# Attended values behind the score products: TensorE's round of a decoder layer put in a new order

## The reference, cut to what matters

```python
x = x + out(softmax(rope(q) @ rope(k).T / sqrt(8), causal) @ v)     # q, k, v from layernorm(x)
q2 = layernorm(x); s2 = (q2 @ wq) (ctx @ wk).T / dk                 # per head of 8, no softmax
y = layernorm(q2 + (s2 @ (ctx @ wv)) @ wo) * ln_g + ln_b
x = x + y
e = argmax(layernorm(x) @ centroids.T)                              # one expert per token
x = x + gated(expert_e(layernorm(x)))
```

## Time and profile before

| | us |
|---|---|
| median of three runs (lowest, highest) | 590.66 (588.89, 592.01) |
| span of the profiled execution, first to last instruction | 587.3 |
| TensorE busy (products) | 544.2 |
| VectorE busy | 486.7 |
| ScalarE busy | 490.9 |
| GpSimd busy | 423.8 |

### The profile page before, as it was taken

The page is one execution under the profiler, slowest core; times in us unless marked ns, Lnnn a source line. Parts: engine busy times, 40 slices in busy tenths (PEclk is TensorE's granted clock), DMA queues, the critical chain, the costliest instruction groups (busy, mean ns, idle before and its releaser), DMA issues.

```text
span 587.3 us, 25042 instructions
## 1 busy us (share of the span) xinstructions
PE 544.2 (93%) x7951; PEld 417.9 (71%) x7951; DVE 486.7 (83%) x1762; ACT 490.9 (84%) x1358; POOL 423.8 (72%) x820
## 2 busy tenths in 40 slices
PE   3889999999999999999999999998889999999994
PEld 2557676767666666666676667665688898899994
DVE  2887898999898989988999898986778777777773
ACT  2778788999888899888898889887688797899993
POOL 3334678888888888888888888777767666454553
PEclk9999999999999999999999999998999999999998
DMA  5521111123111132111221111111211222322210
GB/s 172 69 73 30 30 39 39 57 71 96 59 57 57 58 91 77 58 57 57 64 82 45 39 39 39 46 38 31 70 36 52 67 67 81 91 71 69 68 55 10
DMA packets 55182, 35.35 MB, mean 60 GB/s; under 512 B 14976, under 2 KB 50433, under 8 KB 55056
## 3 DMA queue, kind: packets, MB, share of 16 engines
q1 hardware_dynamic: 50160, 24.44, 15.2%
q0 software_dynamic: 4320, 8.66, 4.5%
q10 hardware_dynamic: 576, 0.66, 0.4%
HBM read 24.46 MB, written 9.74 MB: 58 GB/s over the span
## 4 chain that ended last, share of the span: by engine, by line
PE 79%; issue 6%; ACT 5%; DVE 5%; SPq 1%; POOL 1%; DVEq 1%; DMA 0%; POOLq 0%; ACTq 0%
PE side L946 9%; PE side L747 6%; PE quad L695 6%; PE quad L728 5%; PE quad L733 5%; PE side L808 5%; PE quad L931 4%; PE side L931 4%; PE side L676 4%; PE side L666 3%; PE side L844 3%; PE side L862 3%; PE quad L687 3%; PE side L778 2%; PE side L829 2%
## 5 line engine op out<-in xcount | busy, mean ns | idle before, releaser
L2026 POOL DMA_INDIRECT out<-yo,rb x71 | 70.1, 988 | 59.9 <-DVE yo L1767 53.1
L1055 ACT ACTIVATE ex<-qk,cf 128x512 f32<-128x512 f32 x128 | 85.3, 715 | 0.8
L946 PE MATMUL side<-w,hT 128*128 x568 | 76.7, 278 | 6.2 <-DVE hT L1561 4.7
L1419 DVE TENSOR_REDUCE mx<-quad 128x16 f32<-128x1024 f32 x64 | 75.3, 1218 | 6.6 <-PE quad L695 5.5
L1993 POOL DMA_INDIRECT expert_rows<-pay,sli x64 | 68.6, 1072 | 13.4 <-issue 12.6
L946 PEld LDWEIGHTS side<-w,hT 128*128 128x128 f32 x568 | 69.1, 192 | 9.0 <-issue 8.9
L1071 ACT ACTIVATE prob<-quad 128x1024 f32<-128x1024 f32 x64 | 62.3, 1030 | 1.5 <-PE quad L733 1.5
L1551 DVE TENSOR_SCALAR xh<-rb 128x128 f32<-128x128 f32 x71 | 26.0, 368 | 26.5 <-issue 22.5
L747 PE MATMUL side<-prob,vau 128*32 128x64 f32 x2048 | 41.7, 222 | 4.0 <-issue 2.4
L1168 ACT COPY w1b<-w 128x512 f32 x71 | 43.5, 615 | 0.0
L747 PEld LDWEIGHTS side<-prob,vau 128*32 128x32 f32 x2048 | 31.9, 110 | 10.2 <-issue 3.1
(11 more groups left out here) (270 smaller groups left out, 1641.1 us busy)
## 6 DMA issues: line engine op xcount, KB each, us to landing
rb<-expert_rows SPq DMA_DIRECT2D x71, 68.0 KB, 1.8
xin<-in_x SPq DMA_DIRECT2D x32, 128.0 KB
cin<-in_ctx SPq DMA_DIRECT2D x32, 128.0 KB
xr<-in_x SPq DMA_DIRECT2D x32, 128.0 KB, 2.1
w<-in_w1t SPq DMA_DIRECT2D x8, 256.0 KB
w<-in_w2t SPq DMA_DIRECT2D x8, 256.0 KB
out<-yo,rb POOLq DMA_INDIRECT x71
expert_rows<-pay,sli POOLq DMA_INDIRECT x64, 2.4
```

The lines of the kernel that those rows point to most:

```text
L946: last = mm(YB[u][:, 0:D], hT[u][:, c, :], w2[:, bass.ds(e, 1), c, :], start=c == 0, stop=c == FC - 1)
L1055: act(ex[g.par][:, i, :, :].rearrange("p a t -> p (a t)"), qk[g.par][:, :, :].rearrange("p a t -> p (a t)"), ACT.Copy, scale=own4[:, i:i + ...
L1419: v.tensor_reduce(mx[g.par][:, 2 * h_:2 * h_ + 2, :], quad[:, 2 * h_:2 * h_ + 2, :].rearrange("p r (h k) -> p r h k", k=SQ), AX.X, ALU.max ...
L2026: v.indirect_dma_start(out=o_rows, out_offset=bass.IndirectOffsetOnAxis(ap=number, axis=0), in_=yo[b.c % 4][:, :], in_offset=None, bounds_ ...
```

## The change

Every engine's round gets a new order, and the banks 4 to 7 get new tenants; the instructions of a round stay the same. On TensorE the attended values (64x64 tiles) stand between the score products and the Gram products (64x64 tiles); the two halves of the weighted values stand together at the end; `values` and `ctx_turned` run a round later, `ranks` a round earlier. On ScalarE the round is cut at another place (one more round, most steps one stage deeper), and the second half of `by_head` opens the round. On VectorE `weighted_turned` and `inverse` close the round in which the weighted values are made, and `place` does so for the ranks. GpSimd's two scatters stand side by side. SyncE's queue loads the context two rounds earlier. After the rounds, the steps that now run inside them are dropped, and two waits of the first expert blocks change places.

```diff
         BANK = {
...
+            "x1_turned": bank[5],
+            "cross_keys_values": bank[4],
+            "x_turned": bank[5],
+            "cross_queries": bank[7],
+            "values": bank[6],
+            "ctx_turned": bank[4],
+            "queries_keys": bank[5],
+            "max_rows": bank[7],
+            "projected": bank[6],
...
+            "attended": bank[5],
+            "values_keys0": bank[6],
+            "values_keys1": bank[7],
             "cross_output": bank[4],
+            "ranks": bank[6],
             "weighted": bank[7],
...
@@ SyncE
             def one(g):
-                stage(g, 2, load_ctx)
+                stage(g, 0, load_x)
+                stage(g, 0, load_ctx)
                 stage(g, 3, load_again)
-                stage(g, 0, load_x)
@@ TensorE, the table of waits, first entries of what the text speaks of
-                "attended": [(ac_t, "cT", 4), (ac_f, "xT", 4), (dv_t, "mt", 1), (ac_t, "A", -1)],
+                "attended": [(dv_f, "k2", 4), (ac_f, "xT", 4), (ac_t, "xT", 0), (ac_t, "A", -1)],
-                "x_turned": [(dv_t, "mt", -3), (ac_t, "A", -5), (ac_t, "cT", -1), (ac_f, "xT", -1)],
+                "x_turned": [(ac_t, "xT", -4), (ac_t, "A", -5), (dv_f, "k2", -1), (ac_f, "xT", -1)],
+                "ranks": [(dv_t, "mt", 3), (dv_t, "x1", 2), (ac_f, "V1", 4), (dv_r, "tot", -1)],
+                "weighted": [(dv_t, "mt", 0), (ac_s, "x", 0), (ac_t, "Q2", -2), (dv_a, "ot", -1)],
...
@@ TensorE
             def one(g):
                 stage(g, 4, max_scores)
-                stage(g, 2, x_turned)
                 stage(g, 6, x1_turned)
                 stage(g, 4, cross_keys_values)
-                stage(g, 8, ranks)
+                stage(g, 2, x_turned)
                 stage(g, 6, cross_queries)
-                stage(g, 2, ctx_turned)
+                stage(g, 3, values)
+                stage(g, 3, ctx_turned)
                 stage(g, 2, queries_keys)
-                stage(g, 6, attended)
                 stage(g, 4, max_rows)
                 stage(g, 5, projected)
                 stage(g, 4, scores)
+                stage(g, 6, attended)
+                stage(g, 4, values_keys)
                 stage(g, 6, cross_output)
-                stage(g, 4, values_keys)
+                stage(g, 7, ranks)
                 stage(g, 4, weighted, 0)
-                stage(g, 2, values)
                 stage(g, 4, weighted, 1)
@@ ScalarE
             def one(g):
+                stage(g, 3, by_head, (2, 3))
+                stage(g, 5, norm_x1)
+                stage(g, 6, squares)
+                stage(g, 1, norm_x)
+                stage(g, 5, x1_turned)
+                stage(g, 7, exp_affinity)
+                stage(g, 3, cross_keys_values)
+                stage(g, 1, x_turned)
+                stage(g, 5, cross_queries)
+                stage(g, 3, max_high)
+                stage(g, 2, values)
+                stage(g, 2, ctx_turned)
+                stage(g, 3, max_by_head)
+                stage(g, 6, token_ids)
+                stage(g, 2, by_head, (0, 1))
+                stage(g, 3, exp, 0)
                 stage(g, 5, attended)
-                stage(g, 3, exp, 0)
                 stage(g, 3, exp, 1)
-                stage(g, 0, norm_x)
-                stage(g, 4, norm_x1)
-                stage(g, 5, squares)
-                stage(g, 1, values)
-                stage(g, 0, x_turned)
-                stage(g, 5, token_ids)
-                stage(g, 4, x1_turned)
-                stage(g, 2, cross_keys_values)
-                stage(g, 4, cross_queries)
-                stage(g, 6, exp_affinity)
-                stage(g, 2, max_high)
-                stage(g, 0, ctx_turned)
-                stage(g, 1, by_head, (0, 1))
-                stage(g, 2, max_by_head)
-                stage(g, 1, by_head, (2, 3))
...
@@ VectorE, the new order
+                stage(g, 8, counted)
+                stage(g, 8, own_rank)
                 stage(g, 4, row_max, 0)
+                stage(g, 8, slots)
                 stage(g, 4, row_max, 1)
+                stage(g, 8, alpha)
                 stage(g, 5, turned_back)
+                stage(g, 7, scaled_scores)
                 stage(g, 8, slot_numbers)
                 stage(g, 7, x2_sum)
...
                 stage(g, 7, affinities)
                 stage(g, 7, stats_x2)
                 stage(g, 2, rotate)
                 stage(g, 7, largest)
+                stage(g, 5, x1_sum)
+                stage(g, 7, largest_at)
+                stage(g, 5, stats_x1)
+                stage(g, 7, first_of_them)
+                stage(g, 4, own_head)
+                stage(g, 7, choose)
+                stage(g, 2, partners)
                 stage(g, 6, y_sum)
+                stage(g, 7, place)
+                stage(g, 1, stats_x)
+                stage(g, 4, weighted_turned)
+                stage(g, 4, inverse)
...
@@ GpSimd
             def one(g):
+                stage(g, 1, std_x)
+                stage(g, 6, std_y)
                 stage(g, 4, divide)
-                stage(g, 6, std_y)
+                stage(g, 2, rotated)
                 stage(g, 3, max_low)
-                stage(g, 0, std_x)
                 stage(g, 7, scatter_rows, 0)
-                stage(g, 4, std_x1)
                 stage(g, 7, scatter_rows, 1)
                 stage(g, 6, std_x2)
+                stage(g, 6, row_scalars)
+                stage(g, 5, offset_x1)
+                stage(g, 4, std_x1)
                 stage(g, 5, gain)
-                stage(g, 1, rotated)
-                stage(g, 5, offset_x1)
                 stage(g, 6, scaled_affinity)
-                stage(g, 6, row_scalars)
```

More of the change, by code:

```diff
@@ L432, in decoder_kernel @@
             "max_scores3": bank[3],
-            "x_turned": bank[6],
-            "x1_turned": bank[4],
-            "cross_keys_values": bank[7],
-            "ranks": bank[5],
-            "cross_queries": bank[4],
-            "ctx_turned": bank[6],
-            "queries_keys": bank[7],
-            "max_rows": bank[4],
-            "projected": bank[5],
-            "attended": bank[6],
+            "x1_turned": bank[5],
[7 more added lines that the diff above has]
+            "projected": bank[6],
             "scores0": bank[0],
@@ L446, in decoder_kernel @@
             "scores3": bank[3],
+            "attended": bank[5],
+            "values_keys0": bank[6],
+            "values_keys1": bank[7],
             "cross_output": bank[4],
-            "values_keys0": bank[5],
-            "values_keys1": bank[6],
+            "ranks": bank[6],
             "weighted": bank[7],
-            "values": bank[4],
         }
@@ L464, in decoder_kernel @@
         CT = 2
-        SETUP = bank[5]
+        SETUP = bank[7]
         EARLY_AT = (NG - 4, NG - 1, NG, NG + 1, NG + 2, NG + 3)
@@ L585, in _ @@
                 "max_scores3": [(ac_a, "e1", -1), (dv_s, "m1", -1)],
[L586 to L598 removed]
+                "x1_turned": [(ac_t, "A", -1), (dv_f, "k2", 3), (ac_f, "xT", 3), (ac_t, "xT", -1)],
+                "cross_keys_values": [(dv_t, "y1", -3), (ac_t, "cT", 0), (ac_t, "kv", -1)],
+                "x_turned": [(ac_t, "xT", -4), (ac_t, "A", -5), (dv_f, "k2", -1), (ac_f, "xT", -1)],
+                "cross_queries": [(dv_a, "ot", 1), (dv_t, "mt", 1), (ac_s, "x", 1), (ac_t, "Q2", -1)],
+                "values": [(dv_r, "tot", -5), (dv_t, "mt", -2), (dv_t, "x1", -3), (ac_f, "V1", -1)],
+                "ctx_turned": [(ac_t, "kv", -1), (dv_t, "y1", -4), (ac_t, "cT", -1)],
+                "queries_keys": [(ac_f, "xT", 0), (ac_t, "xT", -4), (ac_t, "A", -5), (dv_f, "k2", -1)],
+                "max_rows": [(ac_t, "Q2", -2), (dv_a, "ot", -1), (dv_t, "mt", -1), (ac_s, "x", -1)],
+                "projected": [(ac_f, "V1", 2), (dv_r, "tot", -3), (dv_t, "mt", 0), (dv_t, "x1", -1)],
                 "scores0": [(dv_s, "m0", 0), (ac_a, "e0", -1)],
@@ L923, in hidden @@
                 if b.c == 1:
-                    wait(pe, ac_t, NG - 3, "A")
                     wait(pe, dv_a, NG - 1, "ot")
-                    wait(pe, dv_t, NG - 1, "mt")
+                    wait(pe, dv_r, NG - 4, "tot")
                 if b.c < 2:
@@ L941, in second @@
                 if b.c == 1:
-                    wait(pe, dv_r, NG - 4, "tot")
+                    wait(pe, ac_t, NG - 3, "A")
                 wait_b(pe, "act_relu", b.n)
@@ L957, in _ @@
             x1_turned(g30)
-            ranks(g28)
             transposed(Block(1))
@@ L1214, in _ @@
             act(ea1[0][:, 0:1], half[:, 0:1], ACT.Exp)
-            rounds(one, NG + 2)
+            rounds(one, NG + 3)
             g28, g29, g30, g31 = (Group(NG - k) for k in (4, 3, 2, 1))
@@ L1227, in step @@
                 return e2
-            attended(g29)
-            exp(g31, 0)
-            exp(g31, 1)
             e0, e1 = first_two(Block(0))
@@ L1466, in own_head @@
                 v.tensor_tensor(mt2[g.par][:, :, :, :],
```

(5 more changed lines are left out.)

37 lines of the change are left out of this document (3 added, 34 removed).

## The result

| | kernel before | kernel after |
|---|---|---|
| median of 5 runs, us | 590.0 (588.9 to 592.0) | 605.1 (602.5 to 605.8) |
| span of the profiled execution, us | 587.3 | 600.2 |

The ratio is 1.0246 with a 95% interval of 1.0224 to 1.0268: 15 us slower where 12.8 us faster was forecast. 605 lies outside the range of 565 to 592.

The account below looks back on a forecast made before the run. TensorE was taken to bound the kernel before, GpSimd the changed one. Gains of 10.6 (steady rounds), 2.1 (outer rounds) and 0.9 (end), less 0.8 (start), make 12.8 us: 590.7 to 578 us, range 565 to 592.

Parts of the forecast that it names:

- all three loads keep about a round of lead: SyncE's queue: context load moves to round 0, its buffer is freed one product later; cost put at nothing.
- start term: First rounds: no 3.16 us context wait, but later values and context and more ScalarE work; net loss 0.8 us, bounds 3.
- 11.95 us: GpSimd's queue per round as the next bound: 11.8 us of its own plus 0.13 for the adjacent scatters.
- gain of 0.44: Saving per steady round, from 12.49 to 12.05 us, the latter being GpSimd's 11.95 plus 0.1 jitter.
- The 0.13 for adjacent scatters: GpSimd: issue gap of 0.31 us between side-by-side scatters instead of 0.18, adding 0.13 a round.
- TensorE, 11.5 to 11.6: TensorE's own round in us, from 12.0, with two tile-shape changes fewer (0.37) and no wait before the attended values.
- Rival 3: Adjacent scatters: the second cannot be prepared until the first has left; GpSimd 12.9 to 13.0 a round, 604 us; chance 0.15.
- Rival 2: New waits between engines, such as x's normalisation on ScalarE, eat the gain: round 12.3 to 12.5, 584 to 592 us; chance 0.22.
- Rival 1: TensorE sets the round at 11.6 us if another order closes short gaps in GpSimd's queue: about 565 us; chance 0.13.
- The end: After the last round: ranks and places of one group and a transpose leave the tail, 0.9 us less.
- The seven intervals of build-up and drain: Intervals outside the 24 steady rounds: extra table and constant work; three late rounds gain 0.3 each, 2.1 us in total.
- the steady term: 24 steady rounds, each 0.44 us shorter: 10.6 us less.

Follow-up runs that it names:

- offset_between: Changed kernel with the mask load a round earlier and GpSimd's offset of x1 moved from behind the scatters to ahead of the first: 581.4 us, ratio 0.9856.
- numbers_norm: `numbers_first` plus the edit of `norm_early` (normalisation of x moved ahead): 578.8 us, ratio 0.9823.
- offset_apart: `offset_between` plus the edit of `norm_early`, with the second scatter behind `std_x2`: 580.6 us, ratio 0.9841; with the scatters still adjacent 580.1 us, 0.9835.
- values_aside: Kernel before with `values` ahead of both weighted halves on TensorE instead of between them: 606.6 us, ratio 0.9893.
- norm_early: `mask_early` with VectorE's statistics and GpSimd's inverse deviation of x moved from the head of the round to its end: 604.7 us, ratio 0.9889.
- slot_early: `mask_early` with VectorE's slot numbers ahead of `alpha`, `turned_back` and `scaled_scores`: 604.4 us, ratio 0.9859.
- low_last: Kernel before with `std_x` and `max_low` exchanged on GpSimd, so `max_low` stands directly ahead of the first scatter: 604.3 us, ratio 1.0251.
- mask_early: Changed kernel with SyncE's one-time loads, the mask first, issued a round earlier: 605.3 us, ratio 0.9873; repeated on another chip 592.5 us, 1.0045.
- numbers_first: `mask_early` with VectorE's slot numbers moved from behind `scaled_scores` to ahead of the second row maximum: 587.7 us, ratio 0.9962.

## Why the prediction was wrong

- **"SyncE's queue: all three loads keep about a round of lead, so nothing."** This is the step that cost most. The term was put at nothing, with the buffer "freed one product later"; in fact the load runs two rounds earlier and `ctx_turned` one round later. The three loads did keep enough lead; the fourth transfer behind them, the mask, did not, and VectorE's queue behind the mask paid. 1.0246 against 1.0045 and 1.0026 on chips where the kernel before takes 590: 12 to 13 us of the 15. Two independent remedies, of the load and of its reader, give the same time within 1.3 us, so it is VectorE's wait and not the transfer's traffic. Without the mask's part the kernel is still 1.5 to 2.8 us above the one before, which is no change that can be told: the gain is missing as well. My start term, a net loss of 0.8 with bounds of 3, came out at nothing for the first group (20.7 in both), and it priced no later group.
- **GpSimd "11.95 us".** The engine was right and the term mis-sized. I listed what stands in its queue and priced the second scatter's gap, but asked only what was ahead of the first scatter on GpSimd, not when its numbers arrive. They arrive 0.23 behind the end of GpSimd's own subtraction, since `scaled_scores` ahead of them is held under it, and the scatter wants 0.82 more. The missed term is 0.85 - 0.18 = 0.67 us a round, and 11.95 + 0.67 is the 12.62 measured. `offset_between` fills it and `numbers_norm` removes its cause; they bring the round to 12.15 and 12.10 against 12.05 predicted. With it in place the gain of 0.44 became a loss of 0.12 to 0.14 in the steady rounds, 12.62 to 12.63 against 12.49 to 12.50.
- **The 0.13 for adjacent scatters.** The gap came as read in the earlier trace rows, 0.30, but `offset_apart` shows that it costs nothing in sum. With the gap closed GpSimd's round is 12.07 to 12.10, some 0.12 to 0.15 above 11.95. The traces show 0.09 of it in one place: `row_scalars` now stands directly behind the power that it needs, and from that power's start to the next instruction are 1.12 us instead of 1.03. The rest is not traced to one instruction.
- **TensorE, 11.5 to 11.6.** Right: 11.5 in the round shown. The wait before attended went, the weighted halves and `values` came out at 1.04 and 0.45. `values_aside` keeps the grouping's part of the gain alone, 1% less time on a chip where the kernel before is slower.
- **Rivals.** Rival 3 had the right engine and threshold (0.67 us of extra on GpSimd cancels the gain) and the right total, 604, by chance: its cause, the second scatter standing over 0.6, did not appear, the first one's gap did, and 12 to 13 us of the total are the mask's. Rival 2 named the normalisation of x on ScalarE: the idle time there is real (0.45 on ScalarE, and through it 0.56 on TensorE) and bound nothing (`norm_early`, no change) until GpSimd's gap was closed; with the numbers early it then gave 9 us, 587.7 to 578.8, since `max_high`, too, came earlier by it. Rival 1 never had a chance with GpSimd at 12.1.
- **The end and the outer rounds.** The end was forecast 0.9 shorter and measured 0.7 longer (175.9 against 175.2). The seven intervals of build-up and drain were forecast 2.1 shorter. In `numbers_norm`, with both faults mended, the first five and the last two together are 1.1 longer than in the kernel before, while the 24 between them are 10.6 shorter: the steady term alone came out as written.

Laid out on the chips of 590: 605.1 as changed; 592.5 with the mask repaired; 578.8 with the slot numbers and the normalisation early, 11 us less than the kernel before. The new order carries the forecast gain in the steady rounds, and two arrivals that it delays take more than it gives. What stays open: the long intervals at the start (in `numbers_norm` 12.6 to 14.7 us until the sixth group, before 11.7 to 13.5), the longer end, neither of which any run took apart, and why `slot_early`'s scatter stands 0.88 behind its last input and the others' 0.82.

## What to carry to other kernels

When a step moves in an in-order queue, follow every instruction behind it in the same round, one-time ones as well, to its first reader; the stall is in the reader's queue. When an engine is to be the new bound, add to its queue the arrival of each input: a full queue turns an input that is 0.7 us late into 0.7 us a round. An idle gap that does not move when other waits disappear is the one to repair, and what pins it can be the engine's own queue: here a small VectorE step held under GpSimd's large one.

## What the runs showed of the hardware

- An indirect scatter on GpSimd starts 0.17 us behind the work ahead of it at best (`offset_between`, `low_last`), not before 0.82 us after the VectorE result on which it waits (`mask_early`, `norm_early`), and not before 0.97 us after the ScalarE result for which the instruction ahead of it waited (`numbers_first`). With only the 0.24 us `max_low` ahead of it the rest of that time is idle; 0.72 us more of work ahead fills it; where the inputs are older, only the 0.17 remains.
- A VectorE instruction on 128x2 (`slot_numbers`, a `tensor_scalar`) took up to 1.22 us instead of 0.16 when it started within GpSimd's 1.27 us subtraction of 128x512 (`slot_early`), and the small `scaled_scores`, with two inputs, 0.82 instead of 0.20 in the changed kernel; both ended with the subtraction in every steady round, whenever they had started. Under GpSimd's 0.69 us power on two columns the same `slot_numbers` took 0.17 (`numbers_first`, `numbers_norm`). The Trainium skill, page "SBUF — State Buffer", section "SBUF: two separate sides", says that a VectorE instruction in a two-port mode or with two SBUF inputs shares a pair of ports with GpSimd's instructions, and that the one of the two that starts first keeps the pair for its whole duration. The trace agrees for both VectorE instructions under the subtraction, and not for `slot_numbers` under the power. Whether `slot_numbers`, with one input, runs in a two-port mode no run here shows.
